# One table of expert sums: a row tile's scatter-addition waits for the tile just ahead only at an expert's first tile, by a count read from memory

## The reference

```python
def _L0_ffn_ref(x, gate_w, gate_b, w1, b1, w2, b2, gamma, beta):
    gate_logits = x @ gate_w + gate_b
    topk_vals, topk_idx = jax.lax.top_k(gate_logits, K)          # K = 2 of E = 16
    topk_w = jax.nn.softmax(topk_vals, axis=-1)
    h = jax.nn.relu(jnp.einsum('bsh,ehf->bsef', x, w1) + b1)
    expert_out = jnp.einsum('bsef,efh->bseh', h, w2) + b2
    sel = jnp.take_along_axis(expert_out, topk_idx[:, :, :, None], axis=2)
    moe = jnp.sum(topk_w[..., None] * sel, axis=2)
    y = x + moe
    ...
    return (y - mu) / jnp.sqrt(var + EPS) * gamma + beta
...
x = x + _L0_ffn_ref(_layernorm(x, axis=-1)[None], ...)[0]
```

## Time and profile before

| | us |
|---|---|
| median of three runs (lowest, highest) | 2166.69 (2164.39, 2167.52) |
| the profiled execution, its own time | 2168.86 |
| its span, first to last instruction | 2167.1 |
| PE busy | 1872.8 (86%) |
| DVE busy | 1393.7 (64%) |
| POOL busy | 1313.3 (61%) |
| ACT busy | 1127.2 (52%) |
| POOL's scatter-additions L884 | 113, 1.56 each |

### The profile page before, as it was taken

How to read it: one execution, slowest core, us unless ns; L and a number is a source line. 1 busy time by engine, 2 the same in 40 slices (tenths; PEclk the granted TensorE clock), 3 DMA queues, 4 the chain that set the end, 5 groups by cost and what they waited for, 6 DMA issues and landing times.

```text
span 2167.1 us, 41905 instructions
## 1 busy us (share of the span) xinstructions
PE 1872.8 (86%) x12047; PEld 1271.7 (59%) x12048; DVE 1393.7 (64%) x3485; ACT 1127.2 (52%) x3220; POOL 1313.3 (61%) x1258
## 2 busy tenths in 40 slices
PE   5676777999999999899999999997766999999950
PEld 3454553565555555455555555555655899999940
DVE  8989998887777777445445555675653544443347
ACT  4765553554454444465655566564642444455534
POOL 2234435777777777777777777772773655544434
PEclk9788887899999999999999999998557999999975
DMA  5333101333333333333333333376764555555575
GB/s 189 108 130 128 30 26 37 100 100 100 100 100 100 100 100 100 105 113 114 112 110 108 110 118 110 110 99 126 235 223 104 101 100 100 104 105 104 105 196 218
DMA packets 150077, 248.13 MB, mean 115 GB/s; under 512 B 25312, under 2 KB 109410, under 8 KB 149922
## 3 DMA queue, kind: packets, MB, share of 16 engines
q0 software_dynamic: 64496, 144.32, 27.5%
q1 hardware_dynamic: 82466, 99.36, 14.5%
q10 hardware_dynamic: 2960, 2.57, 0.4%
HBM read 182.25 MB, written 63.91 MB: 114 GB/s over the span
## 4 chain that ended last, share of the span: by engine, by line
PE 59%; POOL 12%; DVE 12%; issue 7%; DMA 6%; ACT 3%; SPq 0%; DVEq 0%; POOLq 0%; ACTq 0%
PE b L1948 10%; POOL big L855 9%; PE bqk L2231 9%; PE bank L2211 8%; PE bank L2087 4%; PE bqk L2098 4%; DMA big<-xn_dram,big 4%; PE bqk L2003 3%; POOL z_dram L864 3%; PE b L1965 2%; PE bank L1893 2%; PE b L1951 2%; PE bank L1979 2%; DVE st L1235 1%; PE b L2201 1%
## 5 line engine op out<-in xcount | busy, mean ns | idle before, releaser
L855 POOL DMA_INDIRECT big<-xn_dram,big x832 | 827.4, 994 | 265.7 <-issue 225.5
L1948 PE MATMUL b<-big 128*128 128x256 f32 x1468 | 393.7, 394 | 28.2 <-DMA big<-xn_dram,big 25.0
L1948 PEld LDWEIGHTS b<-big 128*128 128x128 f32 x1468 | 260.3, 191 | 191.5 <-issue 106.7
L884 POOL DMA_INDIRECT sum_dram<-mid,idxy x113 | 176.3, 1560 | 231.2 <-ACT mid L1143 129.0
L998 ACT ACTIVATE big<-big 128x128 f32<-128x128 f32 x832 | 265.7, 403 | 37.9 <-PE b L1948 19.4
L2211 PEld LDWEIGHTS bank<-late,mid 128*128 128x128 f32 x1808 | 220.0, 194 | 9.5 <-issue 4.6
L2211 PE MATMUL bank<-late,mid 128*128 128x128 f32 x1808 | 223.9, 278 | 0.0
L2231 PE MATMUL bqk<-big,mid 128*128 x896 | 217.5, 386 | 0.0
L1490 DVE TENSOR_TENSOR acc<-acc,b 128x256 f32 x251 | 104.9, 418 | 153.8 <-PE b L1948 120.5
L1069 ACT ACTIVATE big<-bank 128x512 f32<-128x512 f32 (+1 forms) x208 | 102.4, 578 | 165.5 <-PE bank L2087 165.5
L2231 PEld LDWEIGHTS bqk<-big,mid 128*128 128x128 f32 x896 | 162.2, 191 | 20.8
(11 more groups left out here) (350 smaller groups left out, 3393.4 us busy)
## 6 DMA issues: line engine op xcount, KB each, us to landing
big<-w SPq DMA_DIRECT2D x32, 512.0 KB
mid<-z_dram SPq DMA_DIRECT2D x114, 130.0 KB, 2.1
mid<-b SPq DMA_DIRECT2D x113, 128.0 KB, 3.4
big<-xn_dram,big POOLq DMA_INDIRECT x832
sum_dram<-mid SPq DMA_DIRECT2D x19, 640.0 KB, 4.2
big<-sum_dram SPq DMA_DIRECT2D x18, 640.0 KB, 13.3
acc<-x_pad SPq DMA_DIRECT2D x10, 640.0 KB, 6.4
xn_dram<-big SPq DMA_DIRECT2D x9, 640.0 KB, 3.3
```

The source lines that it names most:

```text
L855: pool.indirect_dma_start(out=gx[t % GB], out_offset=None, in_=xn_dram, in_offset=bass.IndirectOffsetOnAxis(ap=dstA[:, t:t + 1], axis=0)). ...
L884: pool.indirect_dma_start(out=sum_dram[t % 2], in_=yo[t % 4], in_offset=None, out_offset=bass.IndirectOffsetOnAxis(ap=idxy[t % 4][:, 0:1], ...
L1948: a = pe.matmul(to[:, 0:C], wd[t % (2 * EB)], gx[t % GB], start=(e == unit[0] and j == 0), stop=(e == unit[-1] and j == 1), skip_group_che ...
```

## The change

There is one table, `sum_dram`, and every scatter-addition goes to it. It still waits for the landing of tile t - 2. For t from 1 to 4 it also waits for tile t - 1. From t = 5 on POOL reads a number from memory into a register (`lastI[t - 1]`) and waits until the semaphore of tile t - 1's slot has reached it. The number is the full count of tile t - 1 if tile t is its expert's first (`stau` is 0) or lies past the last expert (`etau` is 16 or more), and otherwise 16 less, which is reached already when tile t - 5 has landed. The numbers are worked out by DVE with the other loop tables, from a ramp that POOL writes behind the z scatters. The zero fill of the second table, its loads and the additions L1714 go.

```diff
-        sum_dram = [nc.dram_tensor(f"sum_dram{k}", [NP + P, C], F32).ap() for k in range(2)]
+        sum_dram = nc.dram_tensor("sum_dram", [NP + P, C], F32).ap()
...
+        lastI = acc[0:1, NT - 1, 0:FTL].bitcast(I32)
+        lastb = mid[0:1, 1520:1520 + FTL]
+        firsts = mid[0:1, 1640:1640 + FTL]
...
-                if NU + 2 <= c < 2 * NU + 2:
-                    a = U * (c - NU - 2)
-                    sp.dma_start(sum_dram[1][a * P:(a + U) * P, :].rearrange("(p r) c -> p (r c)", p=P), zero).then_inc(s_zz, 16)
                 if c == 2 * NU + 2:
-                    for k in range(2):
-                        sp.dma_start(sum_dram[k][NP:NP + P, :], zero[:, 0:C]).then_inc(s_zz, 16)
+                    sp.dma_start(sum_dram[NP:NP + P, :], zero[:, 0:C]).then_inc(s_zz, 16)
...
-                for k, a in ((0, zc[u]), (1, z1[u])):
-                    sp.dma_start(a[:, 0:n, :], unit_rows(sum_dram[k], u, n)).then_inc(s_zl[load_group(u)], 16)
+                sp.dma_start(zc[u][:, 0:n, :], unit_rows(sum_dram, u, n)).then_inc(s_zl[load_group(u)], 16)
...
+            pool.iota(lastb[0:1, 0:FT + 3].rearrange("o (i k) -> o i k", k=4), [[16, (FT + 3) // 4], [0, 4]], base=0,
+                      channel_multiplier=0, allow_small_or_imprecise_dtypes=True).then_inc(s_dz, 1)
             pool.wait_ge(s_gb, 16)
+            pool.wait_ge(s_tab, 2)
             for k in range(3):
                 pool.wait_ge(s_zst[k], ZST[k])
             for t in range(FT):
                 pool.wait_ge(f_ys, t + 1)
                 if t >= 2:
                     pool.wait_ge(s_ysc[(t - 2) % 4], 16 * ((t - 2) // 4 + 1))
-                pool.indirect_dma_start(out=sum_dram[t % 2], in_=yo[t % 4], in_offset=None,
+                if 1 <= t < 5:
+                    pool.wait_ge(s_ysc[t - 1], 16)
+                if t >= 5:
+                    landed = pool.value_load(lastI[0:1, t - 1:t], min_val=16, max_val=16 * FTL)
+                    pool.wait_ge(s_ysc[(t - 1) % 4], landed)
+                    pool.sem_inc(s_here, 1)
+                pool.indirect_dma_start(out=sum_dram, in_=yo[t % 4], in_offset=None,
                                         out_offset=bass.IndirectOffsetOnAxis(ap=idxy[t % 4][:, 0:1], axis=0),
                                         compute_op=ALU.add).then_inc(s_ysc[t % 4], 16)
...
-                v.wait_ge(s_zl[load_group(u)], 32 if u < 2 else 64)
-                link(v.tensor_tensor(zc[u][:, 0:n, :], zc[u][:, 0:n, :], z1[u][:, 0:n, :], ALU.add))
+                v.wait_ge(s_zl[load_group(u)], 16 if u < 2 else 32)
                 row_stats(lambda j: zc[u][:, j, :], u, n)
...
-            v.wait_ge(s_zz, 16 * (NU + 2))
+            v.wait_ge(s_zz, 16)
...
             link(v.tensor_tensor(stau, tau[0:1, :], stau, ALU.subtract))
+            mark(v.tensor_scalar(firsts, stau, 0.0, None, ALU.is_equal))
             mark(v.tensor_scalar(expI, etau[0:1, :], float(X - 1), None, ALU.min))
             link(v.tensor_scalar(eregR, etau[0:1, :], float(R), None, ALU.mult))
+            mark(v.scalar_tensor_tensor(out=firsts, in0=etau[0:1, :], scalar=float(X), in1=firsts, op0=ALU.is_ge, op1=ALU.max))
             link(v.scalar_tensor_tensor(out=rowI, in0=stau, scalar=float(P), in1=eregR, op0=ALU.mult, op1=ALU.add))
+            v.wait_ge(s_dz, 5)
+            link(v.scalar_tensor_tensor(out=lastI[0:1, 0:FT], in0=firsts[0:1, 1:FT + 1], scalar=16.0, in1=lastb[0:1, 0:FT],
+                                        op0=ALU.mult, op1=ALU.add))
             v.sem_inc(s_tab, 1)
```

More of the change, by code:

```diff
@@ L455, in program @@
         zc = [big[:, U * C * u:U * C * (u + 1)].rearrange("p (u c) -> p u c", u=U) for u in range(NU)]
-        z1 = [big[:, U * C * (NU + u):U * C * (NU + u + 1)].rearrange("p (u c) -> p u c", u=U) for u in range(NU)]
         gamma_b = big[:, 2 * U * C * NU:2 * U * C * NU + C]
@@ L693, in _ @@
                 sp.wait_ge(s_z, u * U + n)
-                sp.dma_start(unit_rows(sum_dram[0], u, n), zt5[u % 3][:, 0:n, 0:C]).then_inc(s_zst[u % 3], 16)
+                sp.dma_start(unit_rows(sum_dram, u, n), zt5[u % 3][:, 0:n, 0:C]).then_inc(s_zst[u % 3], 16)
             sp.wait_ge(s_dz, 4)
```

## The result

The changed kernel takes 2204.05 us (median of four runs, 2201.25 to 2205.98), the kernel before 2167.11 in the same comparison (2164.39 to 2168.38). The ratio is 1.0168, with a 95% interval of 1.0156 to 1.0180: some 37 us slower, where 6.5 were forecast and 2184 was the end of the range. The profiled execution has a span of 2199.5 against 2167.1.

A forecast was written before the change was run, and what follows sets the result against it. It took PE to bound the expert loop's second half and DVE's table signal to delay the first; +10 (serial end) - 5.5 (combine) + 2 (additions of beta) = +6.5, 2173 us as a median, range 2161 to 2184.

The forecast's parts named there:

- The register load: In the loop from t = 5: load and wait start each scatter 1.37 after its weighing, 1.1 later; scatter alone costs 0.
- the slot's 2.2: In the loop: 2.2 us free between a scatter's landing and DVE's next write of its index slot.
- L889 on the table operations: Loop's first half: POOL's addition of beta, moved with the scatter, lies on DVE's table operations; +2 us, bounds -8 and +12.
- The hold to POOL's end: Rival, loop's first half: POOL's addition of beta holds DVE's table operations to its end; +16.5 in all, 2183, chance 0.13.
- The row on which the choice rested: Profile row in the loop: DVE's copy runs 1684.42 to 1685.24 inside a POOL addition of beta, 1683.97 to 1685.80.
- +12: Upper bound, loop's first half: POOL's addition of beta holds the last two table operations for its whole 1.29.
- the sum's +2: Loop's first half: table operations end 0.1 later, half of that a tile, +2 us over 49 tiles.
- The waits for the tile just ahead, at no cost,: In the loop: an expert's first tile scatters some 0.7 late once, inside the index slot's free time; cost 0.
- the sign named last: In the loop: the prediction is also wrong if DVE's cast begins to wait for landings, the 2.2 us being used up.
- The serial end: Loop's end: eight scatters past the last expert each wait for the one ahead, 4.5 apart; last landing 10 later.
- The combine: After the loop: ten loads and ten additions less; 7.6 to first nbias, spacings of 5.65, 5.5 us less in all.
- The parts at no cost: Sort and table set-up: second table's zero fill goes, iota and three small DVE operations come, covered by SP's waits; cost 0.

The follow-up runs named there:

- b_row: The kernel before, with SP's read of the z row moved ahead of its wait for DVE's tables: 2156.18 us, ratio 0.9948.
- b_load: The kernel before, two tables, with a register read and an always fulfilled wait in front of each scatter from tile 5 on: 2198.53 us.
- e_nobeta: The change without POOL's 49 additions of beta, so the output lacks beta: 2199.57 us.
- e_early: The change, with POOL reading the count and waiting on it before it waits for ACT's weighing: 2181.42 us.
- e_row: The change, with SP's read of the z row moved ahead of its wait for DVE's tables: 2192.94 us.
- e_later: The change with three register reads in front of each scatter instead of one: 2213.99 us.

## Why the prediction was wrong

- **The step that failed** is in "The register load": "For the scatter alone 1.1 is inside the slot's 2.2: cost 0". The shift itself was right: 0.28 + 1.06 = 1.34 behind the weighing, 1.37 forecast. That the index slot is the only thing a later scatter can touch was wrong. Its issue lies on DVE's copy; the slower row reads and the later landings of the z load lie just behind it. All three are on the path from the table operations to the next z tile, which the prediction had named as the one that limits the first half. In the second half it took the loop for PE's, as PE was busy for 192.80 of 192.80; but b_row, which shortens that path, takes this half from 3.785 to 3.752 a tile, so the path had no room there. b_load puts 12.6 and 15.0 us of the two stretches on the shift, for which the sum had 0 and the range no bound.
- **L889 on the table operations**: the mechanism was another than the one chosen, the cost was not far off. The hold to POOL's end, held to be unlikely at 0.13, is what happens: 0.90 and 1739.06 above. The row on which the choice rested showed a copy that got in behind a POOL addition; a copy isn't a table operation with two inputs. The rule of the Trainium skill's page "SBUF — State Buffer" that was weighed against it ("Who interferes with whom") was borne out here as to who is held. Its price, +12, was not: L889 costs 6.6 in the change (e_nobeta) and about 7.3 before. That the sum's +2 came near is luck, as what holds what is another.
- **The waits for the tile just ahead, at no cost,** were wrong as well. In e_early a first tile of the second stretch costs 0.54, as a late scatter collides just so. And the sum left out that tiles 1 to 4 wait too, one behind another: the sign named last, DVE's cast waiting for landings, came true there, 5.5 in four casts, and hardly in the rest of the loop, 0.5 in two. In the change the first stretch is 2.6 longer than b_load's, 2.5 of it between tiles 4 and 11; the second is 1.8 longer, no more than traces of the same loop differ.
- **The serial end** was right: 9.0 by the profile, 10 forecast; the scatters of the tiles past the end are 4.4 to 4.8 apart, 4.5 forecast.
- **The combine** was right: 7.62 to the first nbias (7.6), spacings of 5.58 (5.65), a nbias of 2.25 ("up to 2"), 6.1 less in all (5.5).
- **The parts at no cost** (fill, iota, the small DVE operations): nothing in the profile speaks against it; the start of the loop differs between kernels by as much as it could be worth.

What isn't settled is the split of the 15.0 between copy, row read and z load: e_row takes out the row read and gets 8.6, but moves the z load at the same time, and e_later frees copy and row read, but the z load still comes late there and DVE's casts wait for landings besides.

## What to carry to other kernels

A DMA that is moved by a microsecond is a new neighbour for everything that happens there: look not only for who waits for it but for what runs at its new time, its issue, its first microsecond of transfer and the register reads and loads beside it. Put a register read and its wait ahead of the wait that comes last, so that the instruction behind it is released directly; the like edit in SP's queue was worth 11 us in the kernel before, 9.2 of them in the two stretches. And if a table is to be saved, count what the saved work was hiding and what the new order makes serial: here ten loads and ten additions gave 6 us back. To price an instruction that the change moves, take its cost in the kernel before off first: the additions of beta cost as much there as after.

## What the runs showed of the hardware that was not expected

- A register read from memory takes 0.26 to 0.29 us, on SP, but up to 0.65 where it begins 0.51 to 0.87 behind the end of a scatter-addition's issue; it then ends 1.02 to 1.21 after that end, and the later it began, the less it took.
- POOL's issue of an indirect DMA and DVE's copy hold each other: in the change's second stretch a copy that begins 0.51 to 0.73 after the scatter takes 0.82 to 1.04 instead of 0.69, the issue 1.64 instead of 1.55, and the copy ends 0.08 or 0.09 before it (40 tiles). A copy that begins 0.98 after it takes 0.69, and there the issue takes 1.75 (e_early's tile above).
- An indirect DMA behind a wait of its own started 0.28 after the last signal, and 0.72 after another instruction of POOL had taken the wait.
